# Attending x in blocks of 8 rows and 16 pixels in a convolution, attention and normalisation kernel

## What is computed

```python
# layer 0: x is (4, 256, 64, 64), w1 (128, 256, 7, 7), w2 (49, 128, 1, 1)
k = conv(x, w1, padding=6, rhs_dilation=2) + b1
k = conv(k, w2) + b2
attn = softmax(k, axis=1)                       # 49 weights for each pixel
xp = pad(x, 6)
shifts = stack([xp[:, :, 2*u:2*u+64, 2*v:2*v+64] for u in range(7) for v in range(7)], axis=1)
x = einsum('bkchw,bkhw->bchw', shifts, attn)
# layer 1: yc comes from a scan that doesn't depend on x
y = gelu(yc + x * D)
out = x + y
out = (out - mean_c(out)) * rsqrt(var_c(out) + 1e-5) * ln_w + ln_b   # over the 256 channels
```

## Time and profile before

| what | value |
|---|---|
| median of 3 runs | 814.69 us (812.89 to 814.72) |
| the profiled execution | 813.03 us |
| its span, first to last instruction | 810.9 us |
| TensorE busy in the span | 758.2 us (93%) |
| VectorE | 677.6 us (84%) |
| ScalarE | 566.1 us (70%) |
| GpSimd | 191.0 us (24%) |
| mean granted clock of TensorE | 0.983 of full speed |

### The profile page before, as it was taken

The page is one execution under the profiler, slowest core; times in us unless marked ns, Lnnn a source line. Parts: engine busy times, 40 slices in busy tenths (PEclk is TensorE's granted clock), DMA queues, the critical chain, the costliest instruction groups (busy, mean ns, idle before and its releaser), DMA issues.

```text
span 810.9 us, 27182 instructions
## 1 busy us (share of the span) xinstructions
PE 758.2 (93%) x12242; PEld 448.2 (55%) x12242; DVE 677.6 (84%) x867; ACT 566.1 (70%) x917; POOL 191.0 (24%) x102
## 2 busy tenths in 40 slices
PE   4969989999999999999999999999999999997994
PEld 1535545764567545664567545764567455754671
DVE  0898997989888988989888888998888888595765
ACT  2873545768786796678786787678786777568546
POOL 4114113114211341114301431115302421022011
PEclk9979999999999999999999999999999999999988
DMA  9460050001602035201702053201711020201104
GB/s 295 130 105 2 3 93 16 3 1 24 135 4 53 3 77 81 55 2 27 132 2 55 2 107 53 55 2 27 132 27 30 2 53 4 55 2 48 39 22 104
DMA packets 133598, 41.78 MB, mean 52 GB/s; under 512 B 133145, under 2 KB 133226, under 8 KB 133226
## 3 DMA queue, kind: packets, MB, share of 16 engines
q1 hardware_dynamic: 132248, 40.01, 22.2%
q10 hardware_dynamic: 1234, 0.04, 0.1%
HBM read 23.27 MB, written 16.78 MB: 49 GB/s over the span
## 4 chain that ended last, share of the span: by engine, by line
PE 42%; ACT 20%; DVE 17%; issue 5%; POOL 2%; DVEq 0%; ACTq 0%
PE cv L484 20%; PE wk L525 9%; PE wk L544 4%; ACT chs L903 4%; ACT V L860 4%; PE wk L583 3%; POOL chs L371 2%; PE ms L556 2%; DVE o L1507 2%; DVE V L1359 2%; DVE Z L1400 2%; ACT ms L953 1%; DVE XT L1390 1%; DVE chs L1459 1%; DVE o L1520 1%
## 5 line engine op out<-in xcount | busy, mean ns | idle before, releaser
L484 PE MATMUL cv<-V,W 128*32 128x496 f16 (+6 forms) x7840 | 428.2, 374 | 3.6 <-issue 1.9
L484 PEld LDWEIGHTS cv<-V,W 128*32 128x32 f16 (+1 forms) x7840 | 198.8, 96 | 201.4 <-issue 15.3
L860 ACT ACTIVATE V<-R,sc 128x1024 f16<-128x1024 f32 (+1 forms) x88 | 109.6, 1274 | 59.6 <-DVE R L1285 50.7
L346 POOL TENSOR_TENSOR R<-raw 128x1152 f32<-128x1152 f32 x32 | 93.1, 2909 | 205.6 <-DVE V L1359 102.8
L1359 DVE SCALAR_TENSOR_TENSOR V<-R,sc,V 128x1024 f16<-128x1024 f32 (+1 forms) x88 | 115.1, 1328 | 2.6 <-ACT V L860 2.6
L544 PE MATMUL wk<-band,XT 128*128 128x224 f16 (+1 forms) x900 | 97.3, 266 | 0.9
L544 PEld LDWEIGHTS wk<-band,XT 128*128 128x128 f16 x900 | 76.6, 98 | 24.6 <-ACT o L926 6.0
L525 PEld LDWEIGHTS wk<-AT,sel 128*128 128x128 f16 x2368 | 73.5, 100 | 15.0 <-issue 11.0
L525 PE MATMUL wk<-AT,sel 128*128 128x16 f16 x2368 | 77.8, 193 | 0.1
L371 POOL TENSOR_TENSOR chs<-o 128x1024 f32<-128x1024 f32 x14 | 45.1, 3223 | 132.1 <-DVE o L1507 123.1
L1285 DVE SCALAR_TENSOR_TENSOR R<-R 128x1024 f32<-128x1024 f32 (+1 forms) x56 | 70.3, 1287 | 0.0
(11 more groups left out here) (194 smaller groups left out, 916.9 us busy)
## 6 DMA issues: line engine op xcount, KB each, us to landing
raw<-in_x_dram SPq DMA_DIRECT2D x16, 1024.0 KB, 11.3
out_dram<-o SPq DMA_DIRECT2D x28, 512.0 KB, 4.5
w1raw<-in_L_conv_w_dram SPq DMA_DIRECT2D x2, 3136.0 KB, 16.8
out_dram<-o SPq DMA_DIRECT2D x8, 256.0 KB, 3.9
cm<-in_L_conv_Cmat_dram ACTq DMA_DIRECT2D x1, 32.0 KB, 8.3
dcol<-in_L_conv_D_dram ACTq DMA_DIRECT2D x2, 0.5 KB, 10.2
lnw<-in_L_conv_ln_w_dram ACTq DMA_DIRECT2D x2, 0.5 KB, 7.3
lnb<-in_L_conv_ln_b_dram ACTq DMA_DIRECT2D x2, 0.5 KB, 7.4
```

The source lines that it names most:

```text
L346: nc.gpsimd.tensor_tensor(R[buffer][:, :, :, :], rows_of(par, j + 2), rows_of(par, j), ALU.subtract).then_inc(pool_rows, 1)
L484: ins = pe.matmul(to.rearrange("p (w t c) -> p w t c", w=2, c=COLS)[:, :, :, c0:c1], W[:, ws, h * K7 + v, k0:k1], slot(n, a)[:, low, :, t0 ...
L860: nc.scalar.activation(v_array(n, a, 0), array(a), ACT.Identity, scale=sc[:, par, 3:4]).then_inc(vhi, 1)
```

## The change

A tile of x becomes 8 rows x 16 columns, still 128 pixels. Its band reaches 14 rows and 19 columns (16, and 3 across the inner edge), so a row of the band tile is 2 x 19 columns. Spread goes by columns and not by rows: 8 steps of 2 column pairs x 14 rows = 28 matmuls with 16 columns, one of 56 and one of 28 with 8 columns, still 10 steps; `sel` has 13 variants for 7. A call of apply has 18 matmuls: 12 of 11 x 19 and 6 of 3 x 19 columns, 2850 columns in all.

128 pixels of an 8 x 16 block don't lie at one stride in `raw`. So they are loaded from DRAM once more, block by block, into one of three buffers (two of them lie in AT, where its rows are free between spread and the next turned attention, the third is the new tile xs): a block is 8 rows x 32 pixels, both column parities, for two channel halves, so 2 DMAs of 1024 pieces of 128 B and 8 blocks a unit. `fetch_rows` issues them on ScalarE's queue; block g waits until block g - 3 has been turned, and `turn_x` waits for its block. The first three blocks of the first unit are loaded by SyncE. POOL clears only AT's border rows.

The calls stand in new order on TensorE, ScalarE and VectorE. On ScalarE the preload of the table set for Ln moves ahead of the first squares, and the program then has 2 table loads a unit where it had 4. The cut diff (of the reordering only some pieces):

```diff
 TILES = 2 * (ROWS // 4)
-BROWS = 4 + 2 * PAD
+TROWS, TCOLS = 8, 16
+XROWS, XTILES = ROWS // TROWS, COLS // TCOLS
+STAGES = XROWS * XTILES
+BROWS = TROWS + 2 * PAD
+BCOLS = TCOLS + PAD
...
+SPREAD = tuple(((c, None), (c + 1, None)) for c in range(0, TCOLS, 2))
+SPREAD += (((16, 0), (17, 0), (18, 0), (-3, 1)), ((-2, 1), (-1, 1)))
+STEPS = len(SPREAD)
...
-        band = sb("band", [P, 2, TILES, BROWS, COLS], F16)
+        xs = sb("xs", [P, HALVES * TROWS * 2 * TCOLS])
+        band = sb("band", [P, 2, 2 * XROWS, BROWS, 2 * BCOLS], F16)
...
+        stages = [AT[:, w, PAD:PAD + ROWS, :].rearrange("p r c -> p (r c)").bitcast(F32) for w in range(2)] + [xs[:, :]]
+        tile_rows = lambda n, g, h: xv[n // 2, n % 2, h][:, TROWS * (g // XTILES):TROWS * (g // XTILES) + TROWS,
+                                                         2 * TCOLS * (g % XTILES):2 * TCOLS * (g % XTILES) + 2 * TCOLS]
...
             sp.wait_ge(s_gmax, HALVES * GROUPS)
+            for g in range(3):
+                for h in range(HALVES):
+                    sp.dma_start(stage(g)[:, h], tile_rows(0, g, h)).then_inc(xs_in[g], 16)
             load(1, 1, 0)
...
-                for c in range(COLS):
-                    s = c + 1 if c < PAD else c - COLS + 7 if c >= COLS - PAD else 0
-                    f = (BROWS - 1 - r) * COLS + COLS - 1 - c
-                    ins = pe.matmul(spread_bank(m, r)[:, c * TILES:(c + 1) * TILES].rearrange("p (w j) -> p w j", w=2),
-                                    sel[:, s, f:f + P],
-                                    AT[:, :, r:r + 29:4, c], start=True, stop=True)
+                for k, (c, edge) in enumerate(SPREAD[r]):
+                    v = 3 - c if c < PAD else c - 6 if c > TCOLS - PAD - 1 else 0
+                    for row in range(BROWS):
...
+                        ins = pe.matmul(to, sel[:, f:f + P], attention, start=True, stop=True)
...
-                for j in range(ROWS // 4):
-                    r0, r1 = max(4 * j - PAD, 16 * q), min(4 * j + 4 + PAD, 16 * q + 16)
+                for j in range(XROWS):
+                    r0, r1 = max(TROWS * j - PAD, 16 * q), min(TROWS * j + TROWS + PAD, 16 * q + 16)
...
+                    for e in range(XTILES):
+                        to = out_rows[:, r0 - 16 * q:r1 - 16 * q, (COLS - BCOLS) * e:(COLS - BCOLS) * e + BCOLS]
+                        for k, (xl, bl) in enumerate(((0, 0), (1, 0), (0, 1))):
+                            ins = pe.matmul(to, XT[:, xl, 2 * (XTILES * j + e) + w, h, :],
+                                            band[:, bl, XROWS * w + j, r0 - TROWS * j + PAD:r1 - TROWS * j + PAD,
+                                                 BCOLS * e:BCOLS * e + BCOLS],
...
+                k = STAGES * n + g
+                pe.wait_ge(xs_in[k % 3], 32 * (k // 3) + 32)
...
                 apply(m, 3)
+                conv(n, 30, 33)
                 apply(m, 4)
                 apply(m, 5)
-                conv(n, 30, 33)
                 apply(m, 6)
                 apply(m, 7)
-                mean(m, 0)
                 turn_x(n, par, 0)
                 turn_x(n, par, 1)
+                mean(m, 0)
+                turn_x(n, par, 2)
                 conv(n, 33, 40)
-                turn_x(n, par, 2)
+                variance(m, 0)
                 turn_x(n, par, 3)
-                variance(m, 0)
                 conv(n, 40, 45)
...
+            def fetch_rows(n, g):
+
+                k = STAGES * n + g
+                if g < 3:
+                    act.wait_ge(sel_done, STEPS * n)
+                    act.wait_ge(xt_done, STAGES * n)
+                else:
+                    act.wait_ge(xt_done, k - 2)
+                for h in range(HALVES):
+                    act.dma_start(stage(k)[:, h], tile_rows(n, g, h)).then_inc(xs_in[k % 3], 16)
...
                 attended(m, other, 0)
+                fetch_rows(n, 2)
+                fetch_rows(n, 1)
                 attended(m, other, 1)
-                v_high(n, par, 10)
+                gelu(m, 0, 0)
+                attended(m, other, 2)
+                attended(m, other, 3)
+                fetch_rows(n, 0)
                 sum_2(n, par)
-                attended(m, other, 2)
+                gelu(m, 0, 1)
+                attended(m, other, 4)
...
+                table_of_ln()
+                fetch_rows(n, 3)
+                fetch_rows(n, 4)
                 square(m, 0, 0)
+                square(m, 0, 1)
                 turned_x(n, par, 1)
-                square(m, 0, 1)
+                fetch_rows(n, 5)
```

More of the change, by code:

```diff
@@ L202, in conv_seq_kernel, with band_step @@
         last_banks = [wk[:, 0, :], wk[:, 1, :]] + [cv[:, i, :] for i in range(4)]
+        spread_out = lambda m, s: spread_bank(m, s)[:, 0:2 * XROWS * BROWS * 4].rearrange(
+            "p (n e c) -> p n e c", e=2, c=2)
+        edge_out = lambda m, s: spread_bank(m, s)[:, 0:2 * XROWS * BROWS * len(SPREAD[s])].rearrange(
+            "p (n c) -> p n c", c=len(SPREAD[s]))
+        def band_step(low, s):
+            rows = band[:, low].rearrange("p n r x -> p (n r) x")
+            if s < TCOLS // 2:
+                return rows.rearrange("p n (y z) -> p n y z", z=2)[:, :, s:s + 12:11, :]
+            first = TCOLS if s == TCOLS // 2 else TCOLS + len(SPREAD[s - 1])
+            return rows[:, :, first:first + len(SPREAD[s])]
+        sum_of_step = lambda m, s: (spread_out if s < TCOLS // 2 else edge_out)(m, s)
         spread_bank = lambda m, r: last_banks[r % 6] if m == LAST else wk[:, r % 2, :]
@@ L805, in _ @@
             keep_running(2)
-            for r in range(BROWS):
+            for r in range(STEPS):
                 spread(m, r)
@@ L1032, in unit @@
                 turned_x(n, par, 3)
+                fetch_rows(n, 6)
+                scale_shift(m, 0, 0)
+                turned_x(n, par, 4)
+                fetch_rows(n, 7)
+                spread_mean(m, 1)
                 if nxt:
                     v_high(n + 1, other, 1)
[L1035 to L1038 removed]
                 turned_x(n, par, 5)
@@ L1163, in _ @@
             weights_high(4, 8)
-            turned_x(0, 0, 0)
             v_high(0, 0, 4)
             v_high(0, 0, 5)
+            turned_x(0, 0, 0)
+            fetch_rows(0, 3)
             weights_high(8, 10)
+            sum_1(0, 0)
             turned_x(0, 0, 1)
-            sum_1(0, 0)
+            fetch_rows(0, 4)
             v_high(0, 0, 6)
@@ L1228, in _ @@
             scale_shift(m - 1, 1, 1)
-            for r in range(4, BROWS):
+            for r in range(4, STEPS):
                 band_high(m, r)
@@ L1759, in _ @@
             make_y2_minus(0)
+            turned_x_low(0, 0, 1)
             weights_low(6, 7)
```

165 lines of the change are left out of this document (86 added, 79 removed).

## The result

Twenty runs of each kernel: 815.9 us median with the change (812.39 to 819.07), 812.86 before (812.19 to 814.94). The ratio is 1.0032, 95% interval 1.0022 to 1.0042: slightly slower. The forecast was 804 us and faster, so it was wrong in sign. The profiled execution took 814.02 us, 1.9 under the median of its kernel, and its span is 812.0 against 810.9; that of the kernel before took 813.03 us, close to its median. So the traces show 1.1 us of the 3.0 between the medians.

The account below looks back on a forecast made before the run. TensorE was first suspect, with a chain through ScalarE, VectorE and GpSimd beside it as second bound. Units -8.4, tail -1.4, start +0.5 made -9.3 us on 813.03: 804 us; own range 798 to 810, 8-in-10 range 793 to 818.

Parts of the forecast that it names:

- the 1.2 us of gain per unit: Steady unit: taken between 1.6 us gained (issues hidden) and 0.5 lost (in full); 8.4 us over seven units.
- "in full": From T, start of apply(m, 0): issues fully on ScalarE's time; attended(1) ends T+4.4, variance waits 1.5 us, unit loses 0.5.
- hidden replay: From T, start of apply(m, 0): four issues hidden behind attended(0), run to T+2.95; turns end T+41.3, unit gains 1.6 us.
- Rival 2: Issues stand in full in ScalarE's time: +2.6 us, 815.6, no change that can be told; chance 0.17.
- Apply: TensorE's apply calls, eight per unit: 1.35 us each where it was 1.62, saving 2.2 us per unit.
- Spread: TensorE's spread: 320 matmuls become 308 at a floor of 32 ns, 0.4 us less per unit.
- Table: ScalarE: early preload removes two of four table loads per unit; chain to mean(m, 1) 1.28 us shorter, its 1.03 us wait gone.
- Landing: DMA loads: a stage of 2048 packets of 128 B taken to land in 4.5 us, as a store does.
- rival 3: Pieces land late for turn_x(7), from a landing of 5.6 us on: 3 us per unit, 825 us; chance 0.13.
- Start: Kernel start: two transposes move behind the first conv steps, 1.23 us for two calls, of which 0.5 us is charged.
- Tail: Last unit, where nothing covers spread and apply: 0.4 us from spread, 1.0 from apply, 1.4 us gained.
- Rival 1: TensorE alone counts, no wait forms at turn_x(2): 19 us less, 794 us; chance 0.15.

Follow-up runs that it names:

- the half-piece run: Changed kernel with its loads taking four whole rows, 512 pieces of 256 B, not 1024 of 128 B; 808.32 us, ratio 0.9936.

## Why the prediction was wrong, point by point

**The failed step is the price of the four issues between attended(0) and attended(1), and with it the 1.2 us of gain per unit.** Both replays took 1.5 us for the four, 0.37 each, the lower of the two bounds that the earlier trace rows gave; the "in full" case too, though it was to be the upper one. They took 2.45 to 2.91 us, 2.85 in the unit shown. Their place was as in the hidden replay: they start with attended(0) (0.66 of its 0.74 us are under them), and attended(1) starts at their end. But it starts at T+4.61 where that replay had T+2.95, and ends at T+5.32, later even than the T+4.4 of the "in full" replay. From there comes the wait of 1.11 us at the fourth apply call, where the replays had none and 0.5.

**The reason given for the hidden end did not reach these four.** I took 1.2 us "near the hidden end", because ScalarE's next instruction starts before the one ahead has ended, and because "the four issues of the chain" stand behind three copies and a table load. That row shows two ACTIVATEs overlapping by a tenth of a microsecond, not 2.85 us of issues between two. And the copies and the table load are ahead of the other group, blocks 3 and 4. The Trainium skill's rule that I had cited for the hidden end ("TensorE: Matmul & The Clock Gate", section "Architectural detail: the array is 16× 32×32, not 1× 128×128": a queue of 8, in strict order) doesn't settle this. What I took from it, that an issue is hidden while work is queued ahead of it, the trace bears out for the two issues of block 0 (443.70, with two evacuations still to run). But for the four there is no such work; and how deep the queue is, no run shows.

**Rival 2 named the mechanism, and its time is in part luck.** It forecast 815.6 us, and the median is 815.9. Its own test, attended(1) later than 1.6 us behind attended(0), came out at 2.98. It had a chance of 0.17, where the only row of issues on ScalarE's own queue (0.48 us back to back) spoke for it. But its 2.6 us are a sum of terms of which two are off: in the traces the steady period is 0.37 us longer (0.5 forecast), the start loses 1.35 (0.5), and the tail gains 4.1 (1.4); the two traces differ by 1.1 us in all, the medians by 3.0. The turns end at T+42.9 in the unit shown (T+43.4 forecast), and the next convolution stands at T+43.3, behind a wait of 0.42 us for VectorE's V that no replay had; in the five other full periods it stands at T+43.5 to 44.3.

**The hidden case was worked out well, for another kernel.** With the issues on SyncE the replay holds: attended(1) starts at T+2.94 (T+2.95 in the replay), the turns end at T+40.9 (469.69 less 428.81) where T+41.3 was forecast, turn_x(2) waiting 0.87 us where 1.4 was, no wait at the variance, none at mean(m, 1). Its ratio of 0.9769 is 794.2 us on the 813.03 that the forecast started from, 10 below 804, mostly because I took 1.2 us of a possible 1.6 per unit, and the unit gains 2.2.

**The terms of the sum.**
- *Apply:* 1.35 us per call forecast, 1.41 measured (5.63 for four, 5.64 for the other four), against 1.62. 1.7 us per unit, not 2.2.
- *Spread:* 56 matmuls in 1.85 us (430.04 less 428.19) are 33 ns each, as said. The last 84, with 8 columns, took 2.29 us up to the next row of the timeline (conv at 433.46): 27 ns, where I gave them no more than the rest. That is 0.4 us per unit that the forecast left out.
- *Table:* right in place and size. The chain is shorter by a load, the wait goes, and alone it is worth 7.4 us. The Trainium skill ("ScalarE: Activation LUTs", section "What ACT_TABLE_LOAD costs") would have had 1380 ns more per load; in the kernel with the table alone the load stands at 450.98 for 1.28 us and the next ACTIVATE at 452.28, so this trace again has no such gap.
- *turn_x(2):* a new wait of 1.4 forecast, 1.24 measured.
- *Landing:* 4.5 us taken, 3.1 measured; rival 3 needed 5.6 and got it only as the longest of all.
- *Start:* 0.5 us charged, 1.35 lost up to the first T (165.10 against 163.75). With the loads on SyncE it is 165.97, and with the old blocks in the new order 166.08, so neither the issues nor the blocks are its cause. The new order at the start is what these have in common, but kernels with the same start differ by 1.6 us there (164.81 to 166.44), so the size stays open.
- *Tail:* 1.4 us gained forecast. From the start of the last spread to the end of the span it is 44.3 us (from 767.70) against 48.4 (from 762.49), 4.1 less: 2.1 up to the start of apply, where I had 0.4, and 2.0 behind it, where I had 1.0. VectorE's pace there is near the 1.42 us per call that I had: two of its arguments (L1970) start at 782.39 and 783.75, 1.36 apart.

**What I did not see:** the wait of up to 1.6 us ahead of the variance in the early units (6.3 in all). The "in full" replay had it (1.5 us), but from the late attended(1) alone. With that delay gone the wait is still there (6.7 in all), and with the second group of four issues moved behind the squares it shows only once (1.9), so it is the second group that keeps it up. Rival 1 ("TensorE alone counts", 794) was wrong as a mechanism even where its time came out: the kernel on SyncE still waits at turn_x(2), and taking that wait away gave nothing.

How the 21 us come about inside a unit can be read by setting the unit shown beside that of the kernel with SyncE's issues, each from its T. The changed kernel is 1.28 us behind where the convolution takes over from the fourth apply call, 1.66 at turn_x(2), 1.94 at the variance and 2.41 at the next unit's convolution. What each of the last eight issues costs by itself stays open. Open too is why runs of the changed kernel spread over 6.7 us where the kernel before spreads over 2.8. The issues' own spread, 0.37 to 1.9 us, may be behind it, as the one long period above suggests; no run tested it.

## What to carry to other kernels

A DMA issue is an instruction of the engine that carries it. Here it took 0.6 us at the median and 0.6 to 0.7 in a group of four. Ask what stands ahead of it and what behind: the two issues behind work that was ready to run cost nothing, while the four behind an instruction for which the engine had itself waited held the next one back by 1.7 us (2.98 less 1.30). The engine's idle time in all says nothing about this. Where a cost is bounded from two sides, work out each case with its own bound, not both with the lower one. Move such issues to an engine with nothing else to do, and keep the other halves of a mixed change: here a table load one step earlier was worth 0.9% with no other edit.

## What the runs showed of the hardware

- An issue of 1024 pieces of 128 B took 0.60 us at the median on ScalarE and 0.58 on SyncE, with single ones up to 1.9 and 2.5; with 512 pieces of 256 B it took 0.53 on ScalarE. The shortest is 0.37 in all three.
- The issue starts while ACTIVATEs ahead of it run or are still to run (438.40 and 443.70 in the changed kernel), but the ACTIVATE behind it waits for its end (attended(1) at 441.30, the issues through at 441.25).
- 128 B pieces were cheaper for the DMA engines than I had it from 256 B ones. ScalarE's queue, in the changed kernel:

```profile
q10 hardware_dynamic: 128114, 16.04, 12.7%
```

  That is 12.7% of 16 engines' 812.0 us over 128114 packets, 12.9 ns each, where the mixed queue of the earlier trace rows had 22. The Trainium skill ("DMA: Bandwidth & Descriptors", "How a descriptor splits into AXI transactions") would have every second of these pieces cost what one of 256 B does; the half-piece run has 17.5 ns for each on the same queue (8.9% of 16 engines' 806.6 us):

```profile
q10 hardware_dynamic: 65650, 16.04, 8.9%
```

  These means can't tell: half of the pieces at 17.5 ns and half at half of it would give 13.1, close to what was measured. The single packets of the trace can. Of the 124960 packets of 128 B on that queue 96% took 13 ns, and 94% of the 62464 of 256 B in the half-piece run took 18. Blocks with an even and with an odd number start 128 B apart in a row of 256 B, so one kind must start off a 256 B boundary; yet the packets of blocks 6 have a mean of 13.0 ns and those of blocks 7 one of 13.1. So the rule doesn't show in the packets' times of these traces.
- The spread's matmuls of 8 columns followed every 27 ns where those of 16 took 33, so the pitch of 32 ns that the prediction called a floor is not one.
